# The clears that GpSimd runs ahead of its scatters of routed rows are taken out of a cross-attention and mixture-of-experts kernel

## What is computed

```
x = x + xattn(layernorm(x), ctx, mask)          # 16 heads, 77 context tokens
h = layernorm(x)
scores = sigmoid(h @ gate_weight.T)             # 32 experts in 8 groups
pick 4 groups of 8 by their best (score + bias), then 6 experts in them
w = 2.5 * score / sum of the 6 scores
routed = sum over the 6:  w * (silu(h @ g.T) * (h @ u.T)) @ down.T
shared = (silu(h @ sg.T) * (h @ su.T)) @ sd.T
x = x + routed + shared
```

## Time and profile before

| | us |
|---|---|
| median of 3 runs | 813.57 |
| lowest, highest | 811.62, 813.82 |
| span of the profiled execution | 809.6 |
| median less that span | 4.0 |
| busy TensorE, VectorE, ScalarE, GpSimd | 734.4, 518.8, 389.1, 536.7 |

### The profile page before, as it was taken

How to read it: one execution, slowest core, us unless ns; L and a number is a source line. 1 busy time by engine, 2 the same in 40 slices (tenths; PEclk the granted TensorE clock), 3 DMA queues, 4 the chain that set the end, 5 groups by cost and what they waited for, 6 DMA issues and landing times.

```text
span 809.6 us, 18582 instructions
## 1 busy us (share of the span) xinstructions
PE 734.4 (91%) x5770; PEld 650.9 (80%) x5770; DVE 518.8 (64%) x1619; ACT 389.1 (48%) x832; POOL 536.7 (66%) x794
## 2 busy tenths in 40 slices
PE   6899999999999999986389999999989999899970
PEld 3788898889888888853169999899989999788860
DVE  5887777777777777755145334666666686646673
ACT  2454544444444444420026666665555665556540
POOL 0116878788788778867400007688978888778875
PEclk9899999999999999877699999999999999999995
DMA  9223334433333322214566558798978899778872
GB/s 290 78 54 105 125 125 131 131 124 115 114 127 130 126 72 85 79 66 145 183 195 183 173 165 244 220 266 241 288 232 264 246 275 270 224 228 252 255 222 84
DMA packets 113919, 140.27 MB, mean 173 GB/s; under 512 B 17103, under 2 KB 100691, under 8 KB 113824
## 3 DMA queue, kind: packets, MB, share of 16 engines
q1 hardware_dynamic: 90568, 84.75, 34.0%
q0 software_dynamic: 18432, 50.36, 20.4%
q10 hardware_dynamic: 4824, 3.99, 1.5%
HBM read 75.98 MB, written 63.06 MB: 172 GB/s over the span
## 4 chain that ended last, share of the span: by engine, by line
PE 31%; POOL 30%; issue 20%; DVE 11%; another core or an unknown queue 3%; DMA 2%; SPq 1%; ACT 1%; DVEq 0%; POOLq 0%; ACTq 0%
POOL rows L509 19%; PE sc_ps L1007 16%; PE bank L1019 8%; POOL work L499 7%; PE sc_ps L991 4%; POOL rstd L519 2%; DVE work L1464 2%; DVE work L1483 2%; DVE firsts L1041 1%; DMA store<-in_x 1%; POOL work L546 1%; DMA work<-tabd 1%; DVE work L1438 1%; DVE work L1157 1%
## 5 line engine op out<-in xcount | busy, mean ns | idle before, releaser
L1007 PE MATMUL sc_ps<-work 128*128 128x128 f32 x1792 | 221.0, 277 | 4.4 <-issue 1.8
L1007 PEld LDWEIGHTS sc_ps<-work 128*128 128x128 f32 x1792 | 210.3, 193 | 6.9 <-issue 4.5
L546 POOL DMA_INDIRECT work<-yrows,dest x192 | 188.5, 982 | 36.1 <-POOL work L499 20.5
L509 POOL DMA_INDIRECT rows<-work,dest x192 | 187.7, 977 | 35.0 <-issue 34.8
L499 POOL MEMSET work<- 128x304 f32 (+1 forms) x366 | 137.3, 375 | 104.7 <-DMA yrows<-work 88.9
L1438 DVE TENSOR_TENSOR work<-work,sc_ps 128x256 f32<-128x256 f32 x112 | 46.9, 419 | 128.9 <-issue 72.5
L1019 PE MATMUL bank<-wdn,work 128*128 x448 | 116.7, 383 | 9.9 <-issue 5.3
L1019 PEld LDWEIGHTS bank<-wdn,work 128*128 128x128 f32 x448 | 76.5, 191 | 18.2 <-issue 12.3
L688 ACT ACTIVATE work<-bank 128x512 f32<-128x512 f32 x112 | 66.8, 597 | 40.6 <-PE bank L1019 22.5
L1464 DVE SCALAR_TENSOR_TENSOR work<-work 128x256 f32<-128x256 f32 x160 | 76.8, 480 | 10.8 <-DMA work<-yrows,dest 7.5
L596 ACT ACTIVATE work<-work 128x1232 f32<-128x1232 f32 x32 | 39.4, 1231 | 91.9 <-DVE work L1157 75.3
(11 more groups left out here) (168 smaller groups left out, 1105.0 us busy)
## 6 DMA issues: line engine op xcount, KB each, us to landing
work<-rows SPq DMA_DIRECT2D x224, 128.0 KB
yrows<-work SPq DMA_DIRECT2D x224, 128.0 KB
wgu<-in_egu SPq DMA_DIRECT2D x16, 512.0 KB
store<-in_x SPq DMA_DIRECT2D x8, 512.0 KB, 10.6
wdn<-in_edn SPq DMA_DIRECT2D x8, 512.0 KB
out<-work SPq DMA_DIRECT2D x32, 128.0 KB
rows<-work,dest POOLq DMA_INDIRECT x192
work<-yrows,dest POOLq DMA_INDIRECT x192
```

Of the source, the lines that this page charges most:

```text
L509: pool.indirect_dma_start(rows[:, :], bass.IndirectOffsetOnAxis(ap=dest[:, t, k:k + 1], axis=0), rowb[:, m, :], None).then_inc(scat[m], 16)
L546: pool.indirect_dma_start(yg[:, g % RG, :], None, yrows[0:n * P, :], bass.IndirectOffsetOnAxis(ap=dest[:, t, k:k + 1], axis=0)).then_inc(l ...
L1007: last = mm(ps8[2 + m % 2][:, (2 * w + g) * P:(2 * w + g + 1) * P], wst[w][m % 2][:, k * 2 * I + g * I:k * 2 * I + (g + 1) * I], xeT[:, m ...
```

## The change

`gap(hold)` is no longer called ahead of a scatter, so 174 clears (6 for each of 29 tiles) and the waits between them go. SyncE's wait for the last of them, the constant `PACED` and the name `hold` go with them. The scatters, their order and their waits stay, as do the clears ahead of gathers.

```diff
-PACED = NT - 3
...
217.22 0.97 POOL L509
-        hold = spare1.rearrange("p a d -> p (a d)")[:, NTB:2 * D]
@@ in SyncE's list, behind the waits for the scatters
-            sp.wait_ge(S_["gap"], TOPK * PACED)
@@ in scatter
                     for k in range(half * TOPK // 2, (half + 1) * TOPK // 2):
-                        if t < PACED:
-                            gap(hold)
                         pool.indirect_dma_start(rows[:, :], bass.IndirectOffsetOnAxis(ap=dest[:, t, k:k + 1], axis=0),
                                                 rowb[:, m, :], None).then_inc(scat[m], 16)
```

## The result

The changed kernel takes **857.29 us** (850.89 to 858.82, four runs) beside 813.6 for the kernel before (811.62 to 813.82, four runs), measured beside it: 1.053 times, with an interval of 1.050 to 1.057. That is 43.7 us more, outside the range. The rival that took place is D, and it cost more than either of its two prices. (In the diff above, the line that begins with 217.22 is a row of the profile and no part of the edit.)

The account below looks back on a forecast made before the run. TensorE was taken to bound a tile, with GpSimd some 1 us over. Gains of 0.7 us in tiles 26 and 27 and 1.4 in the last scatters sum to 2.1, taking 813.57 to 811.5 us; range 809.5 to 822.

Parts of the forecast that it names:

- D: Rival for stage A: scatters in a row make TensorE's signals late and tiles longer; 820.1 or 838 us, chance 0.30.
- its two prices: Rival cost over 24 long tiles of stage A: 8.6 us at 1.18 us of lateness, 26 us at 1.92.
- What bounds the kernel: Middle of stage A: TensorE sets the tile of 10.54 us, and GpSimd has some 1 us over.
- Tiles 0 to 25. The cover is TensorE's time.: Stage A, tiles 0 to 25: the 1.4 us saved only lengthen GpSimd's wait, from 1.0 to 2.4; gain 0.
- my rule: Stage A tiles: a TensorE signal up to about 0.8 us late costs nothing; 1.18 us late costs some 0.36.
- The rule that I set against D: The Trainium skill's statement that a DMA never contends with a compute engine, which would leave this rival no chance.
- The late tiles: Tiles 26 to 31: GpSimd's 1/std is in time again in 26, 27 and 29; gain 0.7 us, bounds 0 and 1.7.
- The drain: Last scatters, change of stages: last scatter starts 1.4 us earlier and others' slow issue ends with it; gain 1.4, bounds 0 and 1.4.
- the hold by VectorE that the prediction weighed: First scatter behind a 1/std held beside VectorE's line 1198, 0.41 us long; the last term would be 1.0, not 1.4.
- "Against" D: Slow issue begins only with the stores of zeros, 3.4 us after the first scatter without a clear; stage A has few DMAs.

Follow-up runs that it names:

- c144: The kernel before with clears of 144 floats instead of 288 ahead of scatters: 823.9 us, ratio 1.019.
- every2_b: The kernel before with a clear ahead of every second scatter only, on a chip of the second sort: 825.3 us, ratio 1.019.
- after: The changed kernel in its first measurement and profile, no clears ahead of scatters: 857.29 us, 1.053 times the kernel before.
- before: The kernel without the change, in its first measurement and profile: 813.6 us.
- all32_b: The kernel before with clears ahead of all 192 scatters instead of 174, on a chip of the second sort: 797.19 us, ratio 0.984.
- after_again: The changed kernel run again unedited, on a chip of the second sort: 854.46 us, 1.054 times the kernel before.
- before_again: The kernel before run again unedited with a profile, on a chip of the second sort: 807.8 us in one run.
- after_c: The changed kernel unedited, as the scale on another chip of the second sort: 848.26 us, 1.049 times the kernel before.

## Why the prediction was wrong, point by point

**What bounds the kernel: half right.** TensorE does set the tile, with GpSimd 1.0 us behind; on the chip of the first sort taking the clears out moved nothing in a tile. I counted GpSimd's clears as work whose only effect is its length. They are also a distance between scatters, and on the chips of the second sort that distance is what lets TensorE's signals through in time.

**"Tiles 0 to 25. The cover is TensorE's time. 1.4 us go into GpSimd's wait. Gain 0."** This is the step that failed. The 1.4 us did go into the wait (1.00 to 3.72 us, of which 1.4 are the clears and the rest the longer tile). But the cover isn't TensorE's time any more: it holds only as long as TensorE's signals come in time, and the prediction let them come as before. The tile grew by 1.44 us; over tiles 6 to 24 the mean is 12.00 instead of 10.62, and by the last 1/std that makes 30.3 us.

**Rival D, the mechanism right, its size wrong.** It was named, with the right place and the right sign, at 0.30, and priced at 8.6 to 26 us against 30 to 36 measured in stage A. Two of its steps were off:

- I followed one signal, the rank matmul's (line 861). That it costs something is right, the price was too high: by my rule (0.8 us free, the rest paid in full) the 1.29 us of c144 and the 1.57 of every2_b make a tile 0.49 and 0.77 us longer, and it is 0.27 and 0.34. And I was right that it may fall behind the burst: in after VectorE waited for it once in stage A. But the matmuls of the shared expert (line 872, 867 after) end in the middle of the burst, and their reader, ScalarE's tanh, had stood busy until 1.77 us behind them. No wait was there to be seen, so I had no row for it. In after it comes with the end of the burst, and the tile is 8.25 + 1.14 + 2.59 us long. (3.14 - 1.77 = 1.37 comes near the loss of 1.44, but by luck: in every second tile the tanh is 1.6 us late, less than 1.77, and the tile as long.)
- The lateness was taken from single rows, 1.18 and 1.92 us. It isn't a fixed delay: the signal given towards the end of six scatters 1.27 us apart comes about 1.1 us after the last of them, wherever its matmul ends. Not all of TensorE's signals are held so long: line 829's matmul ends at 223.94, beside the third scatter of six, and VectorE's line 1174 reads it at 225.22, as soon as its list comes to it. The hold grows along the row of scatters, as far as these rows tell.

**The rule that I set against D.** The stalled engines of after sit in stage A beside GpSimd's indirect DMAs; ScalarE's 1.75 us per tile for a release without a source is a compute engine that comes late beside them, in all three profiles of the change (38.5, 38.9 and 36.7 us in all). The Trainium skill (SBUF — State Buffer, "Who interferes with whom") says that a DMA never contends with a compute engine; it speaks of ports of the memory. As a statement on the time of a signal these traces don't agree with it, and I should not have let it weigh on D.

**The late tiles: right as to the wait.** VectorE's wait for the 1/std, 0.86 and 0.48 us in tiles 26 and 27, is 0.32 in tiles 25 to 27 of after (line 1193 at 339.86, 351.57 and 362.18), and so it is in tile 29. A gain of 0.7 can't be seen: tiles 25 and 26 are themselves 2.2 and 1.1 us longer than before, tile 27 0.5 us shorter.

**The drain: right, and worth nothing.** From the last 1/std to the last scatter it is 396.31 - 364.99 = 31.32 us before and 425.21 - 395.29 = 29.92 after, 1.40 earlier, as reckoned. Such a short piece is lost in the slow stretch, whose length varies more than that (46.8 to 53.4 us in the five profiles of before and after). The reading of that stretch, that scatters without a pause hold others' issue up, was right: all32_b shows it. It should have led further: what costs 8 us there with 18 scatters would be there in each tile.

The first scatter of a tile starts 0.16 us behind line 1193's start (220.60 and 220.44) and takes 1.16 us instead of 1.04. That is in line with the hold by VectorE that the prediction weighed, at 0.1 us rather than 0.4.

**The chances.** "Against" D I had put that slow issue begins only with the zeros. In truth stage A could not have shown it at its full size, since all scatters there had their pause. The one stretch without pauses was the best evidence on hand for what the change would do in stage A, and it was slow. D deserved the most likely place, and its upper price (838) was still 19 us short.

**What stays open.** Why chips differ, and whether it is the chip and not the time. Through what the signals are held: the traces give the time of an update, not its way. Whether the recording of the trace has a part in it: every run here was recorded, and the records differ by sort of chip as well. Of the updates of semaphores that are updated 16 times or more by the engines, the traces of the first sort hold 99 to 100%, all others 72 to 82%. No run settles whether the kernel loses as much without a trace being taken. Why the profiled execution of after lost 9.1 us in stage B and after_again 3.0. Whether a pause between 1.37 and 1.50, or between 1.50 and 1.72 us, would be better than 1.50.

## What to carry to other kernels

An instruction that does nothing useful between two DMAs may be a distance, so before it goes, ask what stands beside it, and look for the one stretch of the profile where it is already missing. An engine that isn't waiting for a signal may still have no more than its own list as cover: note for each signal across engines by how much it may come late, not only the waits that there are. And measure on several chips: the clear of one float costs nothing on one (0.997) and 7% on another (1.067).

## What the runs showed of the hardware

- Indirect DMAs issued by GpSimd 1.27 us apart (0.96 us each, 0.30 between) delay semaphore signals from TensorE to ScalarE and VectorE and the issue of SyncE's DMAs on chips of one sort: the tanh that needs a signal starts 1.1 us after the last of six, up to 3.2 us behind its matmul. At 1.50 us apart the same signal is in time (it may be up to 1.77 us late), at 1.37 a fifth of the loss per tile is left.
- The direct stores of SyncE take 1.0 to 3.0 us each beside a long row of such DMAs (before, before_again, after, after_again) and 0.5 to 0.7 behind them or beside paced ones. In after_c, where the row had a break from 422.85 to 426.42 us, four stores begun at 427.52 took 1.97 us in all: the hold isn't there at the start of a row.
- On a chip of the other sort none of this is seen: each signal of TensorE is recorded 0.01 to 0.05 us behind its matmul, tiles are 10.58 us apart with and without clears, and the kernel before is 782 us instead of 810 to 814.
- A clear of one float costs no time between two indirect DMAs: 1.27 us apart with it and without.
- Without their pause, 192 gathers cost 63 us more on a chip of the second sort.
